# A third decision tree served by fetched rows, and a pipeline that carries the finish of each block into the next one

## The chip, the cores and the metric

One Trainium2 chip; the program runs on one of its NeuronCores. That core has TensorE (PE, 128x128 matmuls into PSUM), VectorE (DVE), ScalarE (ACT), GpSimd (POOL), and SyncE (SP), which here only issues DMAs. Each engine has its own instruction stream, in order, and the streams meet only at semaphores. The metric is the device time of one execution in microseconds (us): 1904.74 us for the kernel before, the median of 3 runs (1904.01 to 1905.8).

## The reference, cut to what matters

```
x = x + attn(layernorm(x))                  # x: 8192 tokens x 512
x = x + ffn(layernorm(x))

attn: q, k, v = x W^T + b, each turned into its unit spectrum f / (|f| + eps)
      out = ifft( cumsum_over_tokens(k_hat * v_hat) * conj(q_hat) )

ffn:  logits = x @ W_in.T + b_in            # 8 trees x 255 nodes
      decisions = logits > 0, acts = silu(logits)
      for d in range(7): follow the decision from the current node to a child
      dmap = one-hot of the 8 nodes visited in each tree (7 inner, 1 leaf)
      out = (acts * dmap) @ W_out.T
```

Only 8 of a tree's 255 nodes count for a token. The 127 inner logits are needed to find the path; of the 128 leaves only one is used.

## The kernel before

The 8192 tokens go through in 32 blocks of 256 (`T`), each as two halves `j` of 128. The first, the last two and the 29 in the middle (a hardware loop) run the same `step(i, attn, nxt)` on every engine; `first()` is the prologue (loading, folding a DFT into the projection weights, splitting all weights into an fp16 high and low part, block 0's attention up to its inverse transform). Each fp32 product is three fp16 matmuls (high*high, high*low, low*high).

In step `i`, with `n = i + 1`, PE does:

- `project(n, q)` for Q, K, V: 144 matmuls of 256 columns into `bank_p`, which yield the next block's spectra;
- `logits(i, t, c)`: for tree `t` 12 matmuls of 256 columns for the inner nodes (`c = 0`) and 12 for the leaves (`c = 1`), into `bank_l[t % 4]`, mixed with `counts(i, t)` (2 matmuls, which add a large negative number to every node off the path). Trees in `GATHERED` have no dense leaves: `counts` leaves in the free half of the bank a mark of the leaf reached, `leaf` and `leaf_rows_of` turn it into a row number, and POOL fetches that leaf's input row, bias and output row from HBM (`fetch`, 2 indirect DMAs a tree and block, one for each half). DVE then does `leaf_dots`, ACT `leaf_silu`, DVE `leaf_add`;
- `down(i, j)`: for each half and each of the `DENSE` column groups (14 here) 3 matmuls of 512 columns, into `bank_l[j]`;
- `transform_back(i)`: the inverse transform of block `n` into `bank_i`, 24 small matmuls.

Meanwhile the others do, for block `i`: `residual` (unfold the transform and add x: DVE), `stats`, `normalise`, `high`/`low` (layer norm and its split, ACT and DVE), two DMA transposes that give `x2t`, the input of `logits(i)`; then for each tree `decide` (DVE), `silu` and `act_high` (ACT), `act_low` (DVE). For block `n` they do `evac_*`, `square`, `root` (ACT), `sum_squares`, `add_eps` (POOL), `q_inverse`, `kv_inverse`, `k_scale` (DVE), `bind` (POOL), `running_sum` (DVE), `unbind`, `z_sums`, `z_low` (POOL); and for block `i + 2` the first layer norm. Nothing but the written order of each engine's list and the semaphores sets the order. `silu` writes to three SBUF buffers (`HELD = 3`), so a logit bank is free again once ACT has read it: `logits` of tree 4 and later wait for `act_ready`. `result` (the sum of `down`, the leaf rows and `x1`) ends DVE's step, and SP then stores it.

## Time and profile before

| | |
|---|---|
| median of the runs | 1904.74 us |
| profiled execution | 1902.03 us, of it 1899.9 us from the first to the last instruction |
| granted TensorE clock | 0.989 of full, on average |
| busy | PE 97%, DVE 82%, ACT 59%, POOL 50% |
| one step in the steady part | 56.3 us, 29 alike |
| the chain that ended last | 90% PE |

The profile comes from one execution. Busy time is given per engine; a group of instructions is named by its source line, engine, operation and tiles. "Idle before" says how long the engine stood just before such an instruction, and which instruction it had waited for. Start times count from the first instruction. Successive instructions overlap a little, so the pitch from start to start is shorter than the length given for one.

### The profile page before, as it was taken

What the parts mean: (1) busy time and instruction counts of PE and PEld (TensorE: products, weight loads), DVE (VectorE), ACT (ScalarE), POOL (GpSimd) and SP (SyncE); (2) the same over time, 40 slices, a digit from 0 to 9 for tenths busy, and PEclk for the clock granted to TensorE, in tenths of its full rate; (3) what the DMA queues carried; (4) which work ended last, traced back from release to release, by engine and by line L of the source; (5) the groups of instructions that cost most, each with busy time, mean ns of one, the idle gap of its engine ahead of it and who ended that gap; (6) DMA issues with size and microseconds to landing.
All of it is one profiled execution on the core that took longest, in us unless ns stands there. A gap on an engine that the chain in (4) does not pass through costs nothing.

```text
span 1899.9 us, 40007 instructions
## 1 busy us (share of the span) xinstructions
PE 1846.0 (97%) x14488; PEld 1389.5 (73%) x14488; DVE 1548.9 (82%) x2938; ACT 1117.4 (59%) x2151; POOL 943.0 (50%) x737
## 2 busy tenths in 40 slices
PE   8499999999999999999999999999999999999978
PEld 6478777778777778877777877777877777787755
DVE  4888888888888888888888888888888888888783
ACT  5666565566565556656556656556655555665643
POOL 1254445564445565444556445556544556545450
PEclk9799999999999999999999999999999999999999
DMA  8032232222133222223222213322223322222312
GB/s 288 12 87 79 68 100 92 74 88 88 55 100 100 70 85 88 73 82 100 79 87 87 85 59 100 98 68 88 88 59 96 100 77 77 88 69 86 89 56 67
DMA packets 181785, 163.18 MB, mean 86 GB/s; under 512 B 140161, under 2 KB 140801, under 8 KB 181761
## 3 DMA queue, kind: packets, MB, share of 16 engines
q1 hardware_dynamic: 163328, 95.48, 17.0%
q0 software_dynamic: 18432, 67.38, 10.7%
q8 instruction: 15, 0.25, 0.1%
q14 instruction: 10, 0.07, 0.0%
HBM read 95.72 MB, written 16.78 MB: 59 GB/s over the span
## 4 chain that ended last, share of the span: by engine, by line
PE 90%; DVE 2%; DMA 1%; ACT 1%; issue 0%; SPq 0%; DVEq 0%; ACTq 0%
PE bank_l L532 31%; PE bank_l L589 30%; PE bank_p L482 23%; PE bank_l L542 3%; PE bank_i L482 2%; DMA arena<-xn_pair 1%; PE bank_i L553 1%; PE bank_i L560 0%; SPq L341 0%; DVE xn_pair L1126 0%; DVE arena L1239 0%; ACT xn_pair L721 0%; ACT arena L794 0%; PE bank_i L559 0%; DVE arena L1249 0%
## 5 line engine op out<-in xcount | busy, mean ns | idle before, releaser
L532 PE MATMUL bank_l<-arena,win_mem 128*128 128x256 f16 x5376 | 625.1, 273 | 16.5 <-DMA arena<-xn_pair 16.5
L589 PE MATMUL bank_l<-wout_mem,arena 128*128 128x512 f16 x2688 | 593.4, 379 | 0.0
L532 PEld LDWEIGHTS bank_l<-arena,win_mem 128*128 128x128 f16 x5376 | 525.0, 98 | 80.5 <-DMA arena<-xn_pair 15.1
L482 PE MATMUL bank_p<-arena,wf_hi 128*128 128x256 f16 x3072 | 505.8, 273 | 2.7 <-ACT arena L740 2.7
L589 PEld LDWEIGHTS bank_l<-wout_mem,arena 128*128 128x128 f16 x2688 | 260.6, 98 | 308.8 <-DVE arena L1226 11.7
L482 PE MATMUL bank_p<-arena,wf_lo 128*128 128x256 f16 x1536 | 419.0, 273 | 0.0
L985 POOL TENSOR_TENSOR arena<-arena 128x512 f32<-128x512 f32 x96 | 121.8, 1269 | 553.1 <-ACT arena L749 553.1
L482 PEld LDWEIGHTS bank_p<-arena,wf_hi 128*128 128x128 f16 x3072 | 299.6, 98 | 37.6 <-ACT arena L740 3.0
L1226 DVE SCALAR_TENSOR_TENSOR arena<-arena,s_act 128x512 f16<-128x512 f32 (+1 forms) x256 | 238.7, 942 | 80.4 <-ACT arena L804 66.3
L794 ACT ACTIVATE arena<-bank_l,bias_in,s_logit 128x256 f32<-128x256 f32 x448 | 229.2, 554 | 121.4 <-PE bank_l L542 121.0
L1219 DVE TENSOR_SCALAR dec<-bank_l,thr,off 128x256 bf16<-128x256 f32 x256 | 136.0, 542 | 92.5 <-PE bank_l L532 91.0
L1066 POOL DMA_INDIRECT arena<-in_leaf_rows,leaf_row x128 | 140.3, 1096 | 109.4 <-issue 70.5
L804 ACT ACTIVATE arena<-arena,s_act 128x512 f16<-128x512 f32 (+1 forms) x256 | 166.6, 664 | 3.2
L482 PEld LDWEIGHTS bank_p<-arena,wf_lo 128*128 128x128 f16 x1536 | 150.5, 98 | 17.5
L1136 DVE RECIPROCAL arena<-arena 128x256 f32<-128x256 f32 x64 | 111.9, 1748 | 61.8 <-POOL arena L990 61.8
L1126 DVE TENSOR_TENSOR xn_pair<-arena,xn_pair 128x512 f16<-128x512 f32 x128 | 143.3, 1142 | 9.5 <-ACT xn_pair L721 9.5
L1239 DVE SCALAR_TENSOR_TENSOR arena<-arena 128x512 f32<-128x512 f32 x128 | 142.7, 1167 | 0.9 <-DMA arena<-in_leaf_rows,leaf_row 0.9
L990 POOL TENSOR_SCALAR arena<-arena,eps_s 128x512 f32<-128x512 f32 x64 | 45.4, 709 | 133.3 <-ACT arena L753 130.3
L1148 DVE RECIPROCAL arena<-arena 128x256 f32<-128x256 f32 x64 | 107.7, 1725 | 1.1
L714 ACT ACTIVATE arena<-arena 128x512 f16<-128x512 f32 x31 | 19.5, 630 | 149.1 <-POOL arena L1030 149.1
L726 ACT ACTIVATE arena<-bank_p,bias_f 128x256 f32<-128x256 f32 x192 | 80.5, 470 | 42.0 <-PE bank_p L482 42.0
L749 ACT ACTIVATE arena<-arena 128x1024 f32<-128x1024 f32 x96 | 101.5, 1057 | 5.3
(175 smaller groups left out, 2500.6 us busy)
## 6 DMA issues: line engine op xcount, KB each, us to landing
arena<-in_x SPq DMA_DIRECT2D x32, 512.0 KB, 3.5
arena<-arena SPq DMA_DIRECT2D x32, 512.0 KB, 2.9
out<-arena SPq DMA_DIRECT2D x64, 256.0 KB, 2.1
wout_mem<-in_w_in_t SPq DMA_DIRECT2D x1, 3584.0 KB, 16.1
arena<-in_w_out_t SPq DMA_DIRECT2D x1, 3584.0 KB, 13.8
arena<-xn_pair SPq DMA_TRANSPOSE x128, 2.8
arena<-in_leaf_rows,leaf_row POOLq DMA_INDIRECT x128, 5.7
win_mem<-in_wq SPq DMA_DIRECT2D x1, 1024.0 KB, 7.5
```

What stands on the lines that cost most here:

```text
L482: mm = pe.matmul(bank, a, b, start=(n == 0), stop=(n == len(pairs) - 1))
L532: mm = pe.matmul(bank_l[t % 4][:, c * T:(c + 1) * T], a[:, k, w:w + P], x2t[:, :, b, k, :], start=(c == 0 and k == 0 and m == 0), stop=((t ...
L589: mm = pe.matmul(bank_l[j][:, :], a[:, m, tok], w[:, m, :], start=(m == 0 and a is a_hi and w is wout_hi), stop=(m == DENSE - 1 and a is a ...
L794: ins = act.activation(acts[:, t % HELD, c * T:(c + 1) * T], bank_l[t % 4][:, c * T:(c + 1) * T], ACT.Silu, bias=bias_in[:, c, t:t + 1], s ...
L804: act.activation(a_hi[:, m:m + wide, :], acts[:, t % HELD, 0:wide * T].rearrange("p (c t) -> p c t", c=wide), ACT.Copy, scale=s_act[:, 0:1 ...
L985: pool.tensor_tensor(mag[:, q].rearrange("p c t -> p (c t)"), sq[:, 0:2].rearrange("p c t -> p (c t)"), sq[:, 2:4].rearrange("p c t -> p ( ...
L1066: pool.indirect_dma_start(fetched[:, g, j, :], None, leaf_rows, bass.IndirectOffsetOnAxis(leaf_row[:, g, j:j + 1], 0)).then_inc(leaf_fetch ...
L1126: dve.tensor_tensor(xn_pair[:, j, 1, :], xn[:, j, :], xn_pair[:, j, 0, :], ALU.subtract).then_inc(done, 1)
L1136: dve.reciprocal(mag[:, Q, h], mag[:, Q, h]).then_inc(rinv_ready, 1)
L1219: dve.tensor_scalar(dec[:, t % HELD, :], bank_l[t % 4][:, 0:T], thr[:, t:t + 1], off[:, 0:1], ALU.is_gt, ALU.mult).then_inc(dec_ready, 1)
L1226: dve.scalar_tensor_tensor(out=a_lo[:, m, :], in0=acts[:, t % HELD, 0:wide * T].rearrange("p (c t) -> p c t", c=wide), scalar=s_act[:, 0:1 ...
L1239: ins = dve.scalar_tensor_tensor(out=row, in0=row, scalar=1.0, in1=xn2[:, j, :], op0=ALU.mult, op1=ALU.mult, accum_out=leaf_dot[:, g, j:j ...
```

## The change: what it does

- `GATHERED` goes from two trees to three: tree 2 loses its dense leaf columns, `DENSE` goes from 14 to 13, and there are 6 indirect DMAs a step instead of 4, and three calls each of `leaf`, `leaf_dots`, `leaf_silu` and `leaf_add`.
- `acts` is gone: `silu` writes back into its PSUM bank, `act_high` and `act_low` read there, and a logit bank is free only when `a_lo_ready` comes.
- The normalised `xn2` lives in PSUM (`bank_i`) too; `keep_row` (ACT) copies it to `kept` for the dot products. The sum of x1 and leaf rows is begun by `begin_total` (ACT) in `bank_l[2]`, `bank_l[3]`.
- DVE's `leaf_add` (3) and `result` (2) of block `i` move from the end of step `i` into step `i + 1`, among `residual`, `stats`, `normalise` and `low`; a `last()` does them for block 31.
- The order of the projections is K, V, Q; SP transposes `x2t` ahead of the loads; `fetch` stands behind `z_sums` and ahead of `z_low` on POOL.
- `down(i, 1)` is called in two pieces, with `transform_back` behind both.
- The prologue does K and V before Q, and applies Q's inverse size to the products.

```diff
-GATHERED = (0, 1)
+GATHERED = (0, 1, 2)
-ROUNDS = ((0, 1),)
+ROUNDS = ((0, 1, 2),)
-Q, K, V, G_IN, G_OUT = range(5)
+K, V, Q, G_IN, G_OUT = range(5)
...
-        xn2 = take(J * D).rearrange("p (j d) -> p j d", j=J)
+        kept = take(J * D).rearrange("p (j d) -> p j d", j=J)
...
-        acts = take(HELD * 2 * T).rearrange("p (r t) -> p r t", r=HELD)
+        xn2 = [bank_i[j][:, :] for j in range(J)]
+        total = [bank_l[2 + j][:, :] for j in range(J)]
...
                 if c == 0 and t >= 4:
-                    pe.wait_ge(act_ready, TREES * i + t - 3)
+                    pe.wait_ge(a_lo_ready, TREES * i + t - 3)
                 elif c == 0 and (not isinstance(i, int) or i):
                     if t < J:
                         pe.wait_ge(y_ready, J * (i - 1) + t + 1)
                     else:
-                        pe.wait_ge(act_ready, TREES * (i - 1) + 5 + t)
+                        pe.wait_ge(leaf_added, LEAVES * i)
...
         def step(i, attn, nxt):                 # PE
                 if attn:
-                    project(n, Q)
                     project(n, K)
                     project(n, V)
+                if attn:
+                    project(n, Q)
                 logits(i, 0, 0)
                 logits(i, 1, 0)
                 counts(i, 0)
+                logits(i, 3, 0)
                 logits(i, 2, 0)
-                logits(i, 2, 1)
-                logits(i, 3, 0)
                 logits(i, 3, 1)
                 counts(i, 1)
+                counts(i, 2)
+                if attn:
+                    nyquist_rows(n)
                 logits(i, 4, 0)
...
-                down(i, 0)
-                down(i, 1)
+                down(i, 0, range(TREES))
+                if attn:
+                    nyquist_sums(n)
+                down(i, 1, range(0, 6))
+                down(i, 1, range(6, TREES))
                 if attn:
                     transform_back(i)
...
+            def keep_row(n, j):                  # ACT
+                act.activation(kept[:, j, :], xn2[j], ACT.Copy).then_inc(xn2_kept, 1)
+            def begin_total(i, j):
+                act.wait_ge(a_lo_ready, TREES * i + 7 + j)
+                act.activation(total[j], x1[:, j, :], ACT.Copy).then_inc(total_begun, 1)
...
-                    ins = act.activation(acts[:, t % HELD, c * T:(c + 1) * T], bank_l[t % 4][:, c * T:(c + 1) * T],
+                    ins = act.activation(bank_l[t % 4][:, c * T:(c + 1) * T], bank_l[t % 4][:, c * T:(c + 1) * T],
...
         def step(i, attn, nxt):                 # ACT, from tree 7 on
+                begin_total(i, 0)
                 if nxt:
+                    std(n + 1, mv1, rs1, ln1_mv, ln1_std)
+                if attn:
+                    z_high(n)
+                if nxt:
+                    shifted(n + 1)
                     high(n + 1, xn1, ln1_done, xn1_hi_ready)
-                act_high(i, 7)
-                if attn:
-                    z_high(n)
                 leaf_silu(i, 0)
                 leaf_silu(i, 1)
+                begin_total(i, 1)
+                leaf_silu(i, 2)
...
         def step(i, attn, nxt):                 # POOL
+                    bind(n)
                     q_unit(n)
-                    bind(n)
-                fetch(i, 1)
-                fetch(i, 0)
-                if attn:
                     unbind(n)
                     z_sums(n)
+                for g in range(LEAVES):
+                    fetch(i, g)
+                if attn:
                     z_low(n, 0)
                     z_low(n, 1)
...
         def step(i, attn, nxt):                 # DVE
+                if begun:
+                    leaf_add(i - 1, 0)
+                residual_of(i, 0)
+                residual_of(i, 1)
+                stats2(i)
+                if isinstance(i, int) and i == 0:
+                    win_low(3)
+                normalise2(i)
+                if begun:
+                    leaf_add(i - 1, 1)
+                low2(i)
+                if begun:
+                    leaf_add(i - 1, 2)
+                    result(i - 1, 0)
+                    result(i - 1, 1)
+                if attn:
+                    kv_denominator(n)
+                    kv_inverse(n, 0)
+                decide(i, 0)
+                if attn:
+                    kv_inverse(n, 1)
+                    k_scale(n)
+                decide(i, 1)
+                decide(i, 2)
+                act_low(i, 0)
+                if attn:
+                    q_inverse(n, 0)
+                    q_inverse(n, 1)
+                act_low(i, 1)
+                if attn:
+                    nyquist_den(n)
+                act_low(i, 2)
...
                 leaf_dots(i, 0)
                 leaf_dots(i, 1)
-                leaf_add(i, 0)
                 if attn:
                     carries(n)
-                leaf_add(i, 1)
-                result(i, 0)
-                result(i, 1)
+                leaf_dots(i, 2)
```

DVE, from the layer norm's statistics of block i to the first work for block n, before and after. L1107/L1192 is `normalise`, L1126/L1198 `low`, L1333 `leaf_add`, L1371 `result`, L1136 `q_inverse`, L1222 the K and V denominator.

```order
L1104 RECIPROCAL rs<-rs 128x2 [waits ln2_std]
L1107 TENSOR_SCALAR arena<-arena,mv,rs 128x512 [waits ln2_rstd]
L1107 TENSOR_SCALAR arena<-arena,mv,rs 128x512
L1126 TENSOR_TENSOR xn_pair<-arena,xn_pair 128x512 [waits xn2_hi_ready] x2
L1135 ISA
L1136 RECIPROCAL arena<-arena 128x256 [waits den_ready]
```

```order
L1189 RECIPROCAL rs<-rs 128x2 [waits ln2_std]
L1192 TENSOR_SCALAR bank_i<-arena,mv,rs 128x512 [waits ln2_rstd]
L1192 TENSOR_SCALAR bank_i<-arena,mv,rs 128x512
L1326 REGISTER_ALU
L1333 SCALAR_TENSOR_TENSOR bank_l<-arena,leaf_act,bank_l 128x512 [waits leaf_added,leaf_act_ready]
L1333 SCALAR_TENSOR_TENSOR bank_l<-arena,leaf_act,bank_l 128x512
L1198 TENSOR_TENSOR xn_pair<-bank_i,xn_pair 128x512 [waits xn2_hi_ready] x2
```

Two `leaf_add` instructions of the block before now stand between `normalise` and `low`.

PE, in the middle of the classification: the matmuls of trees 4 and 5 (L544 `logits`, L554 `counts`, L562 a small product) after the change, and then DVE from `decide` of tree 2 on (L1299 `decide`, L1306 `act_low` of trees 0, 1 and 2, L1216 `q_inverse`).

```order
L544 MATMUL bank_l<-arena,win_mem 128x256 [waits a_lo_ready]
L544 MATMUL bank_l<-arena,win_mem 128x256 x23
L544 MATMUL bank_l<-arena,win_mem 128x256 [waits a_lo_ready]
L544 MATMUL bank_l<-arena,win_mem 128x256 x11
L552 REGISTER_ALU
L554 MATMUL bank_l<-dec,path 128x256 [waits dec_ready]
```

```order
L1299 TENSOR_SCALAR dec<-bank_l,thr,off 128x256 [waits count_full,logit_full]
L1306 SCALAR_TENSOR_TENSOR arena<-bank_l,s_act,arena 128x256 [waits a_hi_ready]
L1216 RECIPROCAL arena<-arena 128x256 [waits den_ready] x2
L1306 SCALAR_TENSOR_TENSOR arena<-bank_l,s_act,arena 128x256 [waits a_hi_ready]
L1241 TENSOR_TENSOR sp_den<-bank_p,eps_sp 128x6 [waits sp_abs_ready]
L1306 SCALAR_TENSOR_TENSOR arena<-bank_l,s_act,arena 128x256 [waits a_hi_ready]
```

Before, tree 4's and 5's matmuls waited for `act_ready`; now tree 5's wait for the second of these `act_low`, which stands behind both reciprocals.

POOL, the end of a step, after the change. L1074 and L1075 are `z_sums`, L1120 `fetch`, L1082 `z_low`.

```order
L1074 TENSOR_TENSOR arena<-arena 128x512 [waits z_prod]
L1075 TENSOR_TENSOR arena<-arena 128x512
L1104 ISA
L1120 DMA arena<-in_leaf_rows,leaf_row 128x1028 [waits leaf_added,leaf_row_ready,consts_done]
L1120 DMA arena<-in_leaf_rows,leaf_row 128x1028
L1104 ISA
L1120 DMA arena<-in_leaf_rows,leaf_row 128x1028 [waits leaf_added,leaf_row_ready,consts_done]
L1120 DMA arena<-in_leaf_rows,leaf_row 128x1028
L1104 ISA
L1120 DMA arena<-in_leaf_rows,leaf_row 128x1028 [waits leaf_added,y_stored,leaf_row_ready,consts_done]
L1120 DMA arena<-in_leaf_rows,leaf_row 128x1028
L1080 REGISTER_ALU [waits z_sum]
```

Before, 4 fetches stood between `bind` and `unbind`; now 6 stand behind `z_sums`, and `z_low` behind them.

## Rows read from the trace of the kernel before

**Rows 1.** Head and first part of the profile's page: share of the span.
```profile
span 1899.9 us, 40007 instructions
PE 1846.0 (97%) x14488; PEld 1389.5 (73%) x14488; DVE 1548.9 (82%) x2938; ACT 1117.4 (59%) x2151; POOL 943.0 (50%) x737
```

**Rows 2.** Waits, whole run: who waited for whom, us, times, longest.
```profile
PE bank_l L532 <- DMA arena<-xn_pair: 16.5, 5, 14.1
PE bank_i L482 <- DVE arena L1399: 6.4, 1, 6.4
```

**Rows 3.** Timeline of PE: start, us, instruction (first, one step, last step).
```profile
109.41 2.78 PE L532 MATMUL bank_l<-arena,win_mem 128*128 128x256 f16 x24
...
938.71 0.38 PE L482 MATMUL bank_p<-arena,wf_hi 128*128 128x256 f16 x2
...
954.43 2.78 PE L532 MATMUL bank_l<-arena,win_mem 128*128 128x256 f16 x24
...
995.02 0.38 PE L482 MATMUL bank_p<-arena,wf_hi 128*128 128x256 f16 x2
...
1856.38 4.47 PE L532 MATMUL bank_l<-arena,win_mem 128*128 128x256 f16 x24 [14.11 <-DMA arena<-xn_pair]
```

**Rows 4.** The chain of waits in order of time: two of its pieces.
```profile
938.87 15.72 PE bank_p L482 x144
...
978.18 15.64 PE bank_l L589 x72
```

**Rows 5.** Timeline of DVE: the same step, and block 31.
```profile
946.42 0.25 DVE L1100 BATCH_NORM_AGGREGATE mv<-st 128x2 f32<-128x6 f32 x2
...
948.03 1.00 DVE L1107 TENSOR_SCALAR arena<-arena,mv,rs 128x512 f32<-128x512 f32 x2
949.33 1.29 DVE L1126 TENSOR_TENSOR xn_pair<-arena,xn_pair 128x512 f16<-128x512 f32 x2 [0.30 <-ACT xn_pair L721]
...
960.22 3.37 DVE L1148 RECIPROCAL arena<-arena 128x256 f32<-128x256 f32 x2
...
972.56 1.39 DVE L1199 TENSOR_TENSOR_SCAN arena<-arena,carry 128x256 f32<-128x256 f32 x2
...
995.61 0.28 DVE L1266 SCALAR_TENSOR_TENSOR arena<-bank_i,sp_z,odd 128x64 f32<-128x64 f32 x1 [0.32 <-ACT odd L906]
...
1851.42 1.29 DVE L1126 TENSOR_TENSOR xn_pair<-arena,xn_pair 128x512 f16<-128x512 f32 x2 [0.24 <-ACT xn_pair L721]
```

**Rows 6.** Timeline of ACT: the same step.
```profile
947.50 0.29 ACT L694 ACTIVATE rs<-mv,ln_eps 128x2 f32<-128x2 f32 x1
...
958.55 0.63 ACT L753 ACTIVATE arena<-arena 128x512 f32<-128x512 f32 x1 [0.22 <-POOL arena L985]
959.20 1.28 ACT L794 ACT_TABLE_LOAD   x1
960.50 0.56 ACT L794 ACTIVATE arena<-bank_l,bias_in,s_logit 128x256 f32<-128x256 f32 x1
```

**Rows 7.** Groups by shape: xcount | busy us, mean ns of one | idle before.
```profile
L1249 DVE SCALAR_TENSOR_TENSOR arena<-arena,leaf_act 128x512 f32<-128x512 f32 x128 | 92.4, 762 | 0.5 <-ACT leaf_act L782 0.4
L761 ACT ACTIVATE on_leaf<-bank_l,one,off_inv 128x256 f16<-128x256 f32 x64 | 35.6, 556 | 74.5 <-PE bank_l L542 74.5
L804 ACT ACTIVATE arena<-arena,s_act 128x256 f16<-128x256 f32 x64 | 31.9, 498 | 0.0
L1226 DVE SCALAR_TENSOR_TENSOR arena<-arena,s_act 128x256 f16<-128x256 f32 x64 | 30.8, 482 | 6.1 <-ACT arena L804 6.1
```

**Rows 8.** Timeline of POOL: unbind, second sum, low part of z; a fetch.
```profile
975.63 1.05 POOL L1066 DMA_INDIRECT arena<-in_leaf_rows,leaf_row  x1 [0.30 <-issue]
976.69 1.28 POOL L1018 TENSOR_TENSOR arena<-arena 128x512 f32<-128x512 f32 x1
...
986.77 2.99 POOL L1037 TENSOR_TENSOR arena<-arena 128x512 f16<-128x512 f32 x2 [0.74 <-ACT arena L714]
```

**Rows 9.** The page's DMA part: us from issue to landing.
```profile
arena<-in_leaf_rows,leaf_row POOLq DMA_INDIRECT x128, 5.7
```

More of the change, by code:

```diff
@@ L310, in build, with steps @@
         out_v = out.rearrange("(b j p) d -> b p j d", j=J, p=P)
-        def steps(eng, first, step):
+        def steps(eng, first, step, last=None):
             first()
@@ L323, in steps @@
             step(NB - 1, False, False)
+            if last is not None:
+                last()
         def chunks(flat):
@@ L376, in first @@
                     transpose(j, xt, xt_ready)
+                for j in range(J):
+                    sp.wait_ge(xn2_lo_ready, j + 1)
+                    transpose(j, x2t, x2t_ready)
             def held(value):
@@ L398, in step @@
                     sp.dma_start(xa, x_v[n + 1]).then_inc(x_loaded, 16)
-                for j, have in enumerate((first, second)):
-                    sp.wait_ge(consts_done, 1)
-                    if not isinstance(i, int) or i:
-                        sp.wait_ge(logit_full, classified)
-                    sp.wait_ge(xn2_lo_ready, have)
-                    if isinstance(i, int) and i == 0:
-                        sp.wait_ge(wout_hi_done, 1)
-                        sp.wait_ge(wout_lo_done, 1)
-                    transpose(j, x2t, x2t_ready)
-                if nxt:
                     for j in range(J):
@@ L416, in step @@
                         transpose(j, xt, xt_ready)
-                for j, have in enumerate((first, second)):
+                if attn:
+                    for j in range(J):
+                        sp.wait_ge(consts_done, 1)
+                        sp.wait_ge(logit_full, classified)
+                        sp.wait_ge(xn2_lo_ready, split2[j])
+                        transpose(j, x2t, x2t_ready)
+                for j in range(J):
                     sp.wait_ge(consts_done, 1)
-                    sp.wait_ge(y_ready, have)
+                    sp.wait_ge(y_ready, results[j])
                     sp.dma_start(out_v[i][:, j, :], y[:, j, :]).then_inc(y_stored, 16)
@@ L1544, in step, with last @@
                     carries(n)
-                leaf_add(i, 1)
-                result(i, 0)
-                result(i, 1)
-            steps(dve, first, step)
+                leaf_dots(i, 2)
+            def last():
+                for g in range(LEAVES):
+                    leaf_add(NB - 1, g)
+                result(NB - 1, 0)
+                result(NB - 1, 1)
+            steps(dve, first, step, last)
 def constants():
```

490 lines of the change are left out of this document (268 added, 222 removed).

## The prediction

> **What bounds the kernel now.** Start with the page's first lines [rows 1]: PE is busy 1846.0 of 1899.9 us, the next engine, DVE, 1548.9. Then ask for the waits [rows 2]: in the whole run PE waited 16.5 us for the transposed input of the classification (`x2t`), 14.1 of them in one place, block 31. So in the steady part PE is packed, and its own work is the bound. The timeline of PE gives the step: from 938.71 to 995.02, 56.31 us [rows 3]. The reader is to see there that no row of that step has an idle time in brackets.
>
> How near are the others? Let T0 be the start of the projections (938.71). `low` starts at 949.33 [rows 5], T0+10.62. Block 31 shows how long it takes from there to the first matmul that reads `x2t`, as nothing else held PE: 1851.42 [rows 5] to 1856.38 [rows 3], 4.96 us. So `x2t` was usable at T0+15.58, and PE came for it at 954.43 [rows 3], T0+15.72. This margin of 0.14 us is the most important number here: whatever is put in front of `low` becomes a wait of PE.
>
> **What the change takes off PE.** A matmul of 256 columns costs 15.72/144 = 0.109 us, one of 512 columns 15.64/72 = 0.217 us [rows 4]. The dense leaves of tree 2 were 12 of the first and 6 (two halves, three products) of the second: 1.31 + 1.30 = 2.61 us a step, 83.5 us over 32 steps. Two more tiny row-number matmuls are below 0.1 us. A packed PE would have a step of 53.7 us.
>
> **Wait one: x2t.** Up to the statistics nothing gets earlier: ACT takes the root for the layer norm only after the third evacuation, which PE paces (947.50 [rows 6], T0+8.8), though the statistics have been there since 946.67 [rows 5]. `normalise` then runs from T0+9.32 for 1.00 us. Now two `leaf_add` instructions follow, 92.4/128 = 0.7 us each [rows 7], 1.4 together, and then `low`. Of this 0.30 hides in DVE's former wait for `high` [rows 5]; so `low` begins 1.1 later, if `normalise` is as fast into PSUM as into SBUF. No row before shows a large DVE write into PSUM. Nearest below is its present half of 1.00 us; nearest above is `leaf_add`'s 0.7. I take 0.15 us a piece more, 0.3 for both, since `leaf_add` is what an instruction of this size costs at the ordinary rate. `x2t` comes at T0+15.58+1.4 = T0+17.0: PE waits 1.3 us, bounds 0.9 to 1.6.
> This agrees with a rule of the Trainium skill (VectorE: DVE Perf Modes, "Why PSUM operands drop a tier"), by which an fp32 instruction with a PSUM operand has no double rate. The trace's 1.00 us for two SBUF `normalise` is the fast side; the slow side has no row here. By the rule the wait is 1.3 us, without it 1.0.
>
> **Wait two: tree 5.** A logit bank is now given back only by `act_low`. The order on DVE is `act_low` 0, both `q_inverse`, `act_low` 1, and PE's first matmul of tree 5 waits for the last. Its time follows from rows, because Q now takes the last place that V had: ACT's last root starts at 958.55 (T0+19.84) [rows 6], held by PE's last projection, not by the logits. Then `leaf` for tree 0, which now stands behind it (pitch about 0.5, long 0.556), table load 1.28 with `silu` right behind (959.20, 960.50 [rows 6]), so `silu` starts at T0+22.25 and ends at T0+22.8; `act_high` 0.50 to T0+23.3; `act_low` pitch 0.40 to T0+23.75 [rows 7]; two reciprocals 3.37 [rows 5] to T0+27.1; `act_low` 0.48 to T0+27.55. When does PE come? Seven groups of 12 logit matmuls (84), 6 of `counts` and 4 small ones lie between `x2t` and tree 5: 94 at 0.109, 10.3 us, so T0+26.0 packed and T0+27.3 behind wait one. The gate at T0+27.55 counts from T0 and swallows the first wait: together they cost 27.55-26.0 = 1.55 us a step. Both ends: 1.0 (the gate vanishes, wait one stays) and 2.2 (`act_high` and the two `act_low` each 0.2 slower from PSUM than their rows from SBUF). I take the rows as they are, since `silu` and `decide` read PSUM already at like lengths.
>
> **Leaf rows and z, the long way round on POOL.** `running_sum` stands behind `act_low` 1 and 2 and `decide` 3 and 4 (0.4 to 0.5 each), so it starts at about T0+29.0 and, at twice 1.39 less their overlap [rows 5], ends at T0+31.65. Then unbind and both sums, 976.69 to 986.03 (986.77 less the 0.74 idle): 9.34 us [rows 8], to T0+41.0. The 6 fetches at 1.05+0.30 us [rows 8] end at about T0+49.2; `z_low`, 2.99, at T0+52.3. PE wants z at the new T0' minus 1.35, about T0+53.9: hidden by 1.6 us. The last fetch is issued at T0+48.1 and lands 5.7 later [rows 9], T0+53.8; its two dot products and then `leaf_add` 0, four instructions at 0.65 to 0.7 [rows 7], end at T0+56.5. With T0' = T0+55.25 the residual starts at T0'+1.25, where it was T0+0.6 (995.61 against 995.02 [rows 5]); the statistics end at T0'+8.6, just ahead of ACT's root at T0'+8.8. So this chain costs nothing, with 0.2 us to spare; each us beyond that reaches `x2t` in full, and PE once it exceeds the 0.25 by which the gate lies behind PE.
>
> **Others.** DVE: two more dot products and two more adds at 0.7 [rows 7], 2.8 us a step, less 0.4 for the narrower `act_low`; its 82% becomes about 88%. It fits, and `result` (now at T0+14.6 to 15.9) frees banks 0 and 1 before PE is there. ACT gains a leaf mask, two `keep_row`, two `begin_total` and, because the first layer norm's root now stands behind the `silu`s, two more table loads: 2.6 us at 1.28 [rows 6]; it falls in the long `down`, where I count ACT ready for the leaf dots at T0+47.2. The Trainium skill (ScalarE: Activation LUTs, "What ACT_TABLE_LOAD costs") adds a drain of 1.38 us to each load. The trace disagrees: after 959.20 the next instruction starts 1.30 later [rows 6], so the load alone counts. The `x2t` transposes leave SP ahead of the loads: no change. `down` in two calls with the transform behind both issues the same list as one; nothing.
>
> **Prologue and ends.** PE started the next block's classification at 109.41 [rows 3], after 6.4 us of waiting for the low part of z [rows 2]. With K and V first, the binding overlaps Q's folding and projection; adding up the list (8 tiles, K, a tile, V, 3 tiles, Q, then running sum, products, reciprocals, z) I estimate the first transform about 9 us earlier. But the output weights' split, which was done before and beside it, now stands inside block 0's classification: ACT's and DVE's eight pieces of about 2 us put some 4.7, 3.3 and 2 us of waits into PE. Net of both about +2 us; bounds -5 and +8. In block 31 no projection covers the chain to `x2t`: 14.1 us [rows 2] becomes about 16, +2.
>
> **Sum**, against the profiled execution (1899.9 span, 1902.03 with what lies around it): -83.5 + 30 x 1.55 (46.5) + 2 + 2 = -33, 1869. The median of the runs was 2.7 above that execution; I forecast 1904.7 - 33 = 1871.7, say 1871.
>
> **Rivals.**
> 1. *The waits vanish, PE stays packed.* The two gates are sums of a dozen pitches; 1.5 us off on both, or a DVE that gets through `q_inverse` sooner, frees PE. For: DVE had no wait in PE's way before. Against: the margin of 0.14 us is measured, and two `leaf_add`s are longer. Time: 1904.7 - 83.5 + 4 = 1825; with half the waits 1848. Chance 0.25 for below 1850.
> 2. *Slower: the row fetches come too late.* Place: POOL between `z_sums` and `z_low`, DVE's dots, and `leaf_add` 0 in front of the residual. The margin is 0.2 us. If the fetches take 1.6 instead of 1.35 us each, or POOL's sums are slowed by DVE's new work, the chain is 1.5 to 3 us late; PE then waits 1.0 to 2.6 us more a step. It decides from 1.1 us a step on: there 53.7+1.55+1.1 reaches 56.3. At 3 us late the time is 1871 + 30 x 2.6 = 1949; at 1.5 late 1900. For: the margin is thin, and six fetches stand in a row. Against: the POOL rows repeat from step to step, and DVE reads more from PSUM than before, so it shares less with POOL. Chance 0.12 for slower.
> 3. *The change does not do what it says*: the transform is not inside the `down` products in PE's list. It costs nothing, since z was to be hidden anyway; no chance of its own.
>
> **Chances.** Forecast (1850 to 1893) 0.60; packed or nearly 0.25; same 0.03; slower 0.12. No change would be within 0.2%, 1901 to 1908.5. Faster 0.85, same 0.03, slower 0.12. The range for 8 in 10: 1826 to 1895; the forecast's own is 1850 to 1893.
>
> **What would show it.** In a steady step of the new profile: 54.5 to 56 us from T0 to T0'; PE waits of about 1.3 us at the first `logits` (released by the DMA transposes) and 0.3 us at tree 5 (released by `act_low`); four table loads a step on ACT; `z_low` ending more than 1 us before the transform; `leaf_add` 0 ending about 1 us after T0'. Wrong is it if PE has no waits there (rival 1), or if the residual starts over 2 us after T0' or PE waits at the transform (rival 2).

## The result: slower, and the profile after

The changed kernel takes 2066.07 us (median of 4 runs, 2062.06 to 2072.64); the kernel before took 1904.38 on the same chip. The ratio is 1.0852, with a 95% interval of 1.0834 to 1.0871. The forecast was 1871 us in a range of 1826 to 1895: the kernel became slower where it was to become faster, and the time is 195 us off.

The page of the changed kernel, its head, its queues and its landings (they answer to [rows 1] and [rows 9]):

```profile
span 2060.4 us, 39784 instructions
PE 1822.3 (88%) x13976; PEld 1359.5 (66%) x13976; DVE 1564.6 (76%) x3130; ACT 1250.3 (61%) x2403; POOL 924.4 (45%) x801
...
q1 hardware_dynamic: 163200, 94.96, 22.1%
q0 software_dynamic: 27648, 101.07, 17.4%
...
arena<-in_leaf_rows,leaf_row POOLq DMA_INDIRECT x192, 8.3
arena<-xn_pair SPq DMA_TRANSPOSE x128, 3.3
```

No engine is busier than before in share; even PE fell from 97% to 88%. So the time is in waits. Note the last two lines: a row fetch now lands after 8.3 us where it took 5.7 [rows 9]. The transposes' median of 3.3 hides the point, since it is taken over all 128. Half of them are for the classification (`x2t`), half for the next block's projection (`xt`), and the stretch below shows that the latter are slow.

The waits of the whole run (who waited for whom: us, times, longest), where [rows 2] had 16.5 and 6.4 us in all for PE:

```profile
DVE arena L1320 <- DMA arena<-in_leaf_rows,leaf_row: 200.2, 35, 8.4
PE bank_p L491 <- DMA arena<-xn_pair: 132.3, 29, 6.4
PE bank_l L544 <- DMA arena<-xn_pair: 64.6, 31, 16.0
```

The third row is the forecast wait for `x2t`. The second is new and was in no part of the forecast: in 29 steps PE waits 4.6 us (132.3/29) for the transposed input of the *projection*, `xt`. The first shows the rows late as well. One step in the timeline, engine by engine (it answers to [rows 3], [rows 5] and [rows 8]). T0, the start of its projections, is 1015.66:

```profile
1015.66 0.39 PE L491 MATMUL bank_p<-arena,wf_hi 128*128 128x256 f16 x2 [1.72 <-DMA arena<-xn_pair]
1033.44 2.79 PE L544 MATMUL bank_l<-arena,win_mem 128*128 128x256 f16 x24 [1.72 <-DMA arena<-xn_pair]
1077.42 0.61 PE L491 MATMUL bank_p<-arena,wf_hi 128*128 128x256 f16 x2 [5.93 <-DMA arena<-xn_pair]
...
1025.28 1.53 DVE L1192 TENSOR_SCALAR bank_i<-arena,mv,rs 128x512 f32<-128x512 f32 x2
1043.23 0.38 DVE L1306 SCALAR_TENSOR_TENSOR arena<-bank_l,s_act,arena 128x256 f16<-128x256 f32 x1
1076.64 0.69 DVE L1320 SCALAR_TENSOR_TENSOR arena<-arena 128x512 f32<-128x512 f32 x1 [8.06 <-DMA arena<-in_leaf_rows,leaf_row]
...
1056.63 1.01 POOL L1120 DMA_INDIRECT arena<-in_leaf_rows,leaf_row  x1
1062.91 1.44 POOL L1120 DMA_INDIRECT arena<-in_leaf_rows,leaf_row  x1 [0.30 <-issue]
...
1062.89 5.37 SPq L348 DMA_TRANSPOSE arena<-xn_pair  x2
```

See how the last three rows lie. POOL issues its six fetches from 1056.63 to 1064.35; SP issues the two transposes at 1062.89, in the midst of them. PE can start with `xt` at 1077.42, 14.5 us after that issue. (Its wait of 5.93 is one of the longer ones; they go from 1.4 to 6.4 us.) The step is 61.76 us long here, and over the 28 steps from 210.96 to 1939.82 it is 61.75 on average (56.31 before). What the DMA engines did in that stretch (1056 to 1078), packets, bytes and landings:

```profile
DMA packets 2976, 3.68 MB, mean 167 GB/s; under 512 B 2208, under 2 KB 2208, under 8 KB 2976
q0 software_dynamic: 864, 3.16, 51.5%
q1 hardware_dynamic: 2112, 0.52, 38.0%
arena<-in_leaf_rows,leaf_row POOLq DMA_INDIRECT x6, 10.7
arena<-xn_pair SPq DMA_TRANSPOSE x2, 13.3
```

And the same view of the kernel before, in the like stretch of its step (970 to 992):

```profile
q0 software_dynamic: 576, 2.11, 28.2%
q1 hardware_dynamic: 2112, 0.52, 10.6%
arena<-in_leaf_rows,leaf_row POOLq DMA_INDIRECT x4, 5.8
arena<-xn_pair SPq DMA_TRANSPOSE x2, 2.7
```

The same two transposes, 2112 packets and 0.52 MB both times, took 10.6% of a 22 us stretch and now take 38.0%. Worked out from these shares of 16 engines, one of their packets took 18 ns before and takes 63 now, while one of the row fetches' went only from 172 to 210. Before, the last fetch was issued at 975.63 [rows 8] and landed 5.7 us later, 3.7 us before SP issued the transposes (984.99).

The waits also cost clock. Three projections (144 matmuls each) that began after waits of 1.72, 5.93 and 5.86 us, in stretches (start and end, length, busy time of each engine, then granted clock, DMA share, GB/s):

```profile
1015.60:1033.40 17.80, 16.06 (x144) 13.92 (x144) 16.91 (x43) 13.57 (x28) 3.24 (x3) 1.00 0.20 47
1077.40:1096.50 19.10, 17.54 (x144) 14.87 (x145) 16.92 (x43) 13.53 (x28) 3.25 (x3) 0.91 0.19 43
1140.40:1160.40 20.00, 18.45 (x144) 15.30 (x144) 16.73 (x43) 13.55 (x28) 3.25 (x3) 0.87 0.18 41
```

After the long wait the first matmuls take 0.61 us a pair where they take 0.39 at the full clock of 2.4 GHz: the granted clock is 0.50 of full in the microsecond from 1077.42, its lower level of 1.2 GHz, and comes back within the projection. In such a step that is 1.5 to 2.4 us (17.54 and 18.45 against 16.06 busy) beside the wait itself. Of the 29 waits at this place, 17 were followed by a first pair at the lower clock: 15 of the 16 from 5.0 us up, 2 of the 13 below.

### The profile page after: what moved, and what is told of

Its sections match the earlier page's. It is cut to its first block and busy times, and to the rows that moved or that the text cites. A ratio compares the mean times of both kernels' runs of the same rounds, so it can differ in the third digit from the quotient of the medians.

```text
span 2060.4 us, 39784 instructions
## 1 busy us (share of the span) xinstructions
PE 1822.3 (88%) x13976; PEld 1359.5 (66%) x13976; DVE 1564.6 (76%) x3130; ACT 1250.3 (61%) x2403; POOL 924.4 (45%) x801
## 5 line engine op out<-in xcount | busy, mean ns | idle before, releaser
L491 PE MATMUL bank_p<-arena,wf_hi 128*128 128x256 f16 x3072 | 553.6, 288 | 134.3 <-DMA arena<-xn_pair 132.3
L544 PE MATMUL bank_l<-arena,win_mem 128*128 128x256 f16 x4992 | 583.7, 274 | 68.3 <-DMA arena<-xn_pair 64.6
L544 PEld LDWEIGHTS bank_l<-arena,win_mem 128*128 128x128 f16 x4992 | 483.7, 99 | 138.2 <-issue 54.3
L1320 DVE SCALAR_TENSOR_TENSOR arena<-arena 128x512 f32<-128x512 f32 x192 | 190.8, 1040 | 200.2 <-DMA arena<-in_leaf_rows,leaf_row 200.2
L834 ACT ACTIVATE bank_l<-bank_l,bias_in,s_logit 128x256 f32<-128x256 f32 x416 | 210.8, 537 | 148.9 <-PE bank_l L554 148.5
L1120 POOL DMA_INDIRECT arena<-in_leaf_rows,leaf_row x192 | 196.1, 1022 | 101.1 <-issue 46.3
L1306 DVE SCALAR_TENSOR_TENSOR arena<-bank_l,s_act,arena 128x512 f16<-128x512 f32 (+1 forms) x256 | 161.2, 631 | 39.5 <-ACT arena L844 39.4
L826 ACT ACTIVATE leaf_act<-leaf_dot,arena 128x1 f32<-128x1 f32 x192 | 43.0, 284 | 219.5 <-DVE arena L1320 214.0
L844 ACT ACTIVATE arena<-bank_l,s_act 128x512 f16<-128x512 f32 (+1 forms) x256 | 156.6, 612 | 5.3
L1299 DVE TENSOR_SCALAR dec<-bank_l,thr,off 128x256 bf16<-128x256 f32 x256 | 134.5, 536 | 20.0 <-PE bank_l L544 14.6
L1216 DVE RECIPROCAL arena<-arena 128x256 f32<-128x256 f32 x64 | 107.3, 1718 | 0.0
L1180 DVE TENSOR_TENSOR xn_pair<-arena,xn_pair 128x512 f16<-128x512 f32 x64 | 46.0, 721 | 78.2 <-issue 73.0
## 6 DMA issues: line engine op xcount, KB each, us to landing
arena<-in_w_out_t SPq DMA_DIRECT2D x1, 3328.0 KB, 13.7
```

The costliest lines, as they stand in the source:

```text
L491: mm = pe.matmul(bank, a, b, start=(n == 0), stop=(n == len(pairs) - 1))
L544: mm = pe.matmul(bank_l[t % 4][:, c * T:(c + 1) * T], a[:, k, w:w + P], x2t[:, :, b, k, :], start=(c == 0 and k == 0 and m == 0), stop=((t ...
L834: ins = act.activation(bank_l[t % 4][:, c * T:(c + 1) * T], bank_l[t % 4][:, c * T:(c + 1) * T], ACT.Silu, bias=bias_in[:, c, t:t + 1], sc ...
L844: act.activation(a_hi[:, m:m + wide, :], bank_l[t % 4][:, 0:wide * T].rearrange("p (c t) -> p c t", c=wide), ACT.Copy, scale=s_act[:, 0:1] ...
L1120: pool.indirect_dma_start(fetched[:, g, j, :], None, leaf_rows, bass.IndirectOffsetOnAxis(leaf_row[:, g, j:j + 1], 0)).then_inc(leaf_fetch ...
L1216: dve.reciprocal(mag[:, Q, h], mag[:, Q, h]).then_inc(rinv_ready, 1)
```

## The experiments

All are edits of the changed kernel. Theory T: the six fetches' bytes and the two `xt` transposes are in the 16 DMA engines at once, and both are late. The rivals are named in each expectation. The kernels of experiments 1 and 5 leave half of each row unfetched and serve only to read the time.

**1. Half rows.**

```
-  indirect_dma_start(fetched[:, g, j, :], None, leaf_rows, ...)
+  # from block 1 on: 514 of a row's 1028 words
+  indirect_dma_start(fetched[:, g, j, 0:ROW // 2], None, leaf_rows.rearrange("r (a w) -> (r a) w", a=2), ...)
```

> The changed kernel, but from block 1 on each of the six row fetches of a step brings 514 of a row's 1028 words (so the leaves' dots and sums are taken over rows that are partly old: the output is not the reference's). The number of fetches, their place on POOL and every instruction elsewhere stay; the bytes fall from 3.16 to 1.58 MB a step. Theory T (the six fetches' bytes share the 16 DMA engines with the two transposes of the next block's rows, which then land after 9 to 14 us, and the projection waits for them 4.6 us a step, with a slower TensorE clock behind it): the projection's wait falls under 1 us a step, the period from 61.8 to 56 to 57.5 us, the whole to about 1900 us (1880 to 1940). Rival A (the new order of the next layer norm's high and low halves and of x2t's transposes makes the transposes late, whatever the traffic): no change, within 10 us of 2066. Rival B (the number of gather instructions on the software queue, not their bytes): no change either, 2040 to 2070.

Measured: 1879.65 us (1872.57 to 1881.12), 0.9869 of before (0.9848 to 0.9891). The larger group of the projection (count, busy us, mean ns, idle before) and the wait at `x2t`:

```profile
L491 PE MATMUL bank_p<-arena,wf_hi 128*128 128x256 f16 x3072 | 509.2, 274 | 5.9 <-DMA arena<-xn_pair 3.9 <-issue 1.9
```

```profile
PE bank_l L544 <- DMA arena<-xn_pair: 63.5, 31, 16.0
```

In the changed kernel this group read 553.6, 288 and 134.3 idle. With six fetches in the same place and every instruction elsewhere kept, only the bytes halved: the projection's wait went from 132.3 to 3.9 us, and its matmuls went back from 288 to 274 ns. In the stretch from 1028 to 1050 the two transposes landed after 4.2 us (median), where they took 13.3. The period is 55.4 us (from `x2t` to `x2t`, 1005.15 to 1060.51). Between the two profiled spans lie 181.5 us: 128.4 less idle time before the projection, and 48.0 less busy time of PE (1822.3 to 1774.3), the clock's part. T holds; rivals A and B would have left the time alone. Time and period came out just below T's ranges (1880 to 1940, and 56 to 57.5).

**2. Fetches ahead of z's products again,** with the next layer norm's high halves ahead of `z_high`:

```
 POOL:  bind; q_unit
+       fetch x6
        unbind; z_sums
-       fetch x6
        z_low
 ACT:   leaf_row_copy behind act_high(3), was behind silu(6); high(n + 1) before z_high(n), was after
```

> The changed kernel with the fetches of the leaf rows back where the kernel before had them, ahead of z's products on POOL (the copy of the row numbers behind the fourth act_high, about T0+30), and the next layer norm's high halves ahead of z_high on ACT. Still three trees by row, six fetches, 3.16 MB. Theory T: fetches are over before the two transposes are issued, which land in about 3 us; the projection does not wait, TensorE's clock stays at 1.00, the period is 55 to 56.5 us, the whole 1860 to 1900 us. Rival A': three trees by row are too many bytes wherever they stand: the transposes still wait, or the rows, and the whole stays over 1950. Rival C: z is late instead, because eight microseconds of POOL stand ahead of its products, and the transform waits: 1920 to 2000.

Measured: 1965.25 us (1953.48 to 1970.65), 1.0340 (1.0323 to 1.0358). The projection's wait is gone and its clock back at 1.00, as T says, but the time lies 65 us above T's range, for another wait. The number falls into the ranges of rivals A' and C, but neither mechanism is there: PE waits for no transpose at the projection and not at all at the transform. What it does wait for:

```profile
DVE dec L1299 <- remote: 80.9, 31, 3.1
PE bank_l L554 <- DVE dec L1299: 64.7, 26, 2.7
```

```profile
1060.49 0.75 DVE L1306 SCALAR_TENSOR_TENSOR arena<-bank_l,s_act,arena 128x512 f16<-128x512 f32 x1 [0.25 <-issue]
1064.23 0.54 DVE L1299 TENSOR_SCALAR dec<-bank_l,thr,off 128x256 bf16<-128x256 f32 x1 [2.99 <-remote]
```

DVE stands still for 3 us (1.6 to 3.1 in other steps) ahead of the eighth tree's comparison, though that tree's last logit matmuls ended at 1060.23, as the row of PE says:

```profile
1058.76 1.47 PE L544 MATMUL bank_l<-arena,win_mem 128*128 128x256 f16 x12
```

The profile can name no releaser ("remote" stands for one that it does not know). The semaphore updates in the trace say more: the comparison waits for a count (a semaphore) that PE's last logit matmul raises, and this count rose only at 1064.21, 3.98 us after the matmul's end (which the profile models) and 0.02 before the comparison. In the 31 steps with this stall the count came 2.3 to 4.0 us late. So VectorE waits for a late count of PE. Experiments 5, 6, 7 and 11 go after it.

**3. The transposes held back until the rows have landed.**

```
 SP, before the xt transposes:
+  sp.wait_ge(leaf_fetched[0..2], 16 * J * (i + 1))
```

> The changed kernel with SP holding the two transposes of the next block's rows back until the step's six row fetches have landed. Theory T (they share the engines, nothing else): the rows land earlier than 10 us after their issue (6 to 8), the transposes 3 to 4 us after theirs, and the projection starts at about the time at which it starts now or up to 3 us earlier: 1980 to 2080 us. Rival A (transposes are issued too late, they are slow for a reason of their own): every transpose still takes 9 us or more from its issue, and the whole rises by 29 times 6 to 8 us, to over 2220.

Measured: 1977.41 us, 1.0395 (1.0374 to 1.0416): 89 us *faster* than the changed kernel, by making the transposes wait, and 3 us below T's range. The rows' landing, and one step (fetches from 1075.28):

```profile
arena<-in_leaf_rows,leaf_row POOLq DMA_INDIRECT x192, 6.3
```

```profile
1075.28 1.01 POOL L1125 DMA_INDIRECT arena<-in_leaf_rows,leaf_row  x1 [0.16 <-issue]
...
1087.92 2.62 SPq L348 DMA_TRANSPOSE arena<-xn_pair  x2
...
1092.50 0.39 PE L496 MATMUL bank_p<-arena,wf_hi 128*128 128x256 f16 x2 [2.36 <-DMA arena<-xn_pair]
```

One after the other, the rows need 12.6 us from the first fetch's issue (1087.92 less 1075.28) and the transposes 4.6 more, 17.2 in all. Side by side they needed 20.8 in the step shown above (1056.63 to 1077.42). Over all steps the same stretch, from the first fetch to the projection, is 17.5 us long here and 19.4 in the changed kernel, where it varies from 16.2 to 21.2. So mixed, they lose 1.9 us on average, though not in every step: "they share the engines, nothing else" is not the whole of it. Rival A falls: a transpose has no slowness of its own.

**4. High halves first, fetches left late.** The ACT edit of experiment 2 alone (`high(n + 1)` ahead of `z_high(n)`).

> The changed kernel with the next layer norm's high halves ahead of z_high on ACT, as in the kernel before; the fetches stay between z's sums and z's low part. Rival A (the transposes are issued too late): they are issued 2 to 3 us earlier, the projection's wait falls from 4.6 to about 2 us and the whole to 1990 to 2010. Theory T: the transposes are issued earlier and fall into the middle of the fetches, and land hardly earlier; the wait stays over 3.5 us and the whole is 2030 to 2070.

Measured: 2067.85 us, 1.0870 (1.0835 to 1.0905), within its spread the changed kernel's time; the projection's wait was 128.6 us. It is what T expected, but a weak test: one step shows the transposes issued 5.85 us after the first fetch (1059.26 less 1053.41) instead of 6.26 (1062.89 less 1056.63), so the edit moved them by 0.4 us and not by the 2 to 3 that I had assumed. They were read 14.7 us after their issue (1073.98), as late as before. So this run does not test rival A; experiment 3 does.

**5. Experiment 2 with half rows.**

> The kernel of the second experiment (row fetches ahead of z's products) with half rows from block 1 on (514 of 1028 words; the output is not the reference's). There the eighth tree's comparison on VectorE started 3 us late in every step (2.99 us idle, released by an unknown queue) and PE waited 2.7 us for it. Theory D (the stall comes of the 3.16 MB on the DMA engines): it is gone or under 0.5 us, the period 55.4 us, the whole 1870 to 1885. Theory G (it comes of GpSimd's issuing six fetches, whose number and time stay): it stays at 2 to 3 us, the period 58, the whole 1950 to 1970.

Measured: 1871.14 us, 0.9834 (0.9814 to 0.9853). No stall at the comparison; PE's waits there are the 6.0 us of the first steps. Theory D holds: the stall of experiment 2 comes with the bytes, not with issuing fetches. PE's count for the eighth comparison rises 0.01 us after its matmul here in every step.

**6. The second sum over leaf rows behind the low halves** (experiment 2's kernel, full rows):

```
 DVE:   normalise2(i)
-       leaf_add(i - 1, 1)
        low2(i)
+       leaf_add(i - 1, 1)
```

> The kernel of the second experiment with the second sum over leaf rows moved behind both low halves of xn2 on VectorE, so that x2t's transposes can be issued some 1.5 us earlier. If the wait of 1.5 us at x2t is made of what stands ahead of these halves, it falls to 0.2 us or less and the period by 1.3 to 1.5: 1915 to 1930 us with the stall at the eighth comparison, 1830 to 1850 if that goes too. If instead something else ends last there (the normalisation into PSUM, the transposes themselves), it stays above 1 us and the time within 10 us of 1965.

Measured: **1864.68 us** (1864.11 to 1866.22), 0.9799 of before (0.9782 to 0.9815). This is the best kernel of the study, 1.9 to 2.2% faster than the kernel before. The stall is gone, with all bytes fetched. PE's waits and, for the step, its rows:

```profile
PE bank_l L544 <- DMA arena<-xn_pair: 25.0, 31, 14.7
PE bank_l L544 <- DVE arena L1306: 18.2, 32, 2.2
PE bank_l L554 <- DVE dec L1299: 15.9, 33, 2.2
```

```profile
995.89 2.79 PE L544 MATMUL bank_l<-arena,win_mem 128*128 128x256 f16 x24 [0.35 <-DMA arena<-xn_pair]
999.00 0.39 PE L554 MATMUL bank_l<-dec,path 128*128 128x256 bf16 x2 [0.32 <-DVE dec L1299]
...
1007.26 1.48 PE L544 MATMUL bank_l<-arena,win_mem 128*128 128x256 f16 x12 [0.52 <-DVE arena L1306]
```

The wait for `x2t` shrank from 1.5 to 0.35 us, as meant; but 0.32 and 0.52 us took its place (the comparison of tree 0, now behind more of DVE's work, and `act_low` 1 at tree 5's gate). The period is 55.27 us (median) where experiment 5, with the `x2t` wait whole, had 55.36. My range for "stall gone" (1830 to 1850) had counted the freed 1.3 us without asking what is late next.

**7. The row numbers' copy one `act_high` later,** in experiment 6's kernel.

> The kernel of the experiment before it with the copy of the row numbers behind the fifth act_high instead of the fourth, so that the six fetches start about 1.8 us later, still ahead of z's products. If the stall of the eighth comparison depends on how much of the traffic has been issued when it comes up, it shrinks to under 1.5 us and the whole falls by 40 us or more against that experiment; if it goes with the end of the fetches' issue, it grows by about 1.8 us and the whole rises by about 50 us. The transposes stay clear of the fetches in both cases (they were landed 4 us before PE came to them): no wait at the projection.

Measured: 1867.92 us, 0.9815 (0.9799 to 0.9831). Neither branch: there was no stall left to shrink or to grow. The fetches started only 1.4 us later (33.5 against 32.1 us behind T0, medians), and the 3 us in all lie within the overlap of the two intervals.

**8. The rows held back until the transposes have landed,** `z_low` ahead of them on POOL.

```
 POOL:  unbind; z_sums; z_low
+       wait_ge(xt_ready, 16 * J * (n + 2))
        fetch x6
```

> The changed kernel with z's low part ahead of the fetches on POOL, and the fetches held back until the two transposes of the next block's rows have landed. Theory T (they slow each other on the shared DMA engines): the transposes land in 3 to 4 us and the projection does not wait (under 0.5 us a step), TensorE starts it at the full clock. The rows land 6 to 8 us after their issue, 10 us or so after the transform's start, the dots, the residual and x2t's transposes behind them on VectorE come 7 to 10 us late, and the wait moves to x2t: 6 to 10 us a step there, the whole 2030 to 2180 us. If the transposes still took 9 us or more with nothing beside them, theory T would be wrong.

Measured: 2228.97 us, 1.1714 (1.1691 to 1.1738), clock 0.92. The transposes took 3.2 us and PE no longer waits for them, as T says. The price of late rows is 49 us above the expected range, and it is paid in another place:

```profile
PE bank_p L491 <- ACT arena L770: 280.9, 30, 10.4
PE bank_l L544 <- DMA arena<-xn_pair: 66.6, 31, 21.2
```

```profile
1025.10 1.28 ACT L826 ACT_TABLE_LOAD   x1 [13.97 <-DVE arena L1322]
...
1033.68 0.82 ACT L770 ACTIVATE arena<-bank_p,bias_f 128x256 f32<-128x256 f32 x2
```

Late rows make late dots, `leaf_silu` stands on ACT ahead of everything of the next step, and ACT waits 13.97 us for them; its first evacuation of the projection's banks starts at 1033.68, and PE, out of banks, waits 9 us. It is not `x2t` that pays, but the projection.

**9. Two trees by row** in the changed kernel's order (four fetches, in the late place; tree 2 dense again).

```
-GATHERED = (0, 1, 2)        -ROUNDS = ((0, 1, 2),)
+GATHERED = (0, 1)           +ROUNDS = ((0, 1),)
```

> The changed kernel with two trees by row instead of three, as the kernel before had, and four fetches (2.11 MB) a step; they stay between z's sums and z's low part. Its x2t transposes of block 0 wait for one more scale, and the third tree's second half of logits is back on TensorE (2.6 us a step). If four fetches also collide with the transposes of the next block's rows, the projection waits 3 us or more and the whole is over 2040 us. If four are over in time (they start 6 us before the transposes and need 6 to 8 us of all engines), the wait is under 1 us and the period 55.4 and 2.6 us, 58: 1935 to 1965 us. That would say that neither the third tree nor the new place costs the 4.6 us alone, only both together.

Measured: 1956.93 us, 1.0283 (1.0263 to 1.0304). Two neighbouring steps:

```profile
926.73 2.79 PE L545 MATMUL bank_l<-arena,win_mem 128*128 128x256 f16 x24 [1.58 <-DMA arena<-xn_pair]
984.71 2.79 PE L545 MATMUL bank_l<-arena,win_mem 128*128 128x256 f16 x24 [1.59 <-DMA arena<-xn_pair]
```

The period is 58.0 us; PE waits 1.6 us a step at `x2t` and not at all at the projection. As expected, four fetches in the late place do no harm: the transposes are issued 7.7 us behind the first fetch, when the last has some 2 us to go, and both have landed 4.7 us later (4.5 in experiment 3). So neither the third tree nor the new place makes the 4.6 us alone. The third tree's dense leaves are 2.6 us of this period; without them it would be 55.4.

**10. Experiment 6's DVE edit alone,** fetches left late.

> The changed kernel with only the second sum over leaf rows behind the low halves of xn2. The wait at x2t goes from 1.5 to about 0.3 us a step. If the projection's start is set by the transposes (which follow the block's own logits on ACT and DVE, all of them shifted with PE), the whole falls by about 30 times 1.2 us less the waits of 0.8 us that took its place in the sixth experiment: 2040 to 2066 us, with the projection's wait still 4 us or more.

Measured: 2072.24 us, 1.0889 (1.0858 to 1.0921), where 2040 to 2066 was expected; it can't be told from the changed kernel's time. The wait for `x2t` fell to 25.3 us in the run and the projection's wait rose to 145.4: as long as the transposes set the step, nothing gained elsewhere counts.

**11. Experiment 2 with the copy one `act_high` later.**

> The kernel of the second experiment, where the eighth comparison on VectorE stalls 3 us in every step, with the row numbers' copy one act_high later (fetches start about 1.8 us later), and the sum over leaf rows not moved. If the stall comes of the full traffic at that instruction whatever its moment, it is there again and the whole is about 1965 us; if it needs a certain moment of the fetches against the comparison, it goes and the whole is 1870 to 1885 us (as with half rows).

Measured: 1915.43 us, 1.0067 (1.0051 to 1.0084): between the two numbers. The stall left DVE and appeared on ACT, ahead of the eighth tree's `silu`:

```profile
ACT bank_l L834 <- remote: 88.6, 29, 3.2
PE bank_l L599 <- DVE arena L1306: 28.0, 28, 1.1
```

3.1 us a step again (88.6/29), but ACT has room there, and PE pays 1.0 us of it. Again it is a count of PE that rises late, this time that of a `counts` matmul: 3.2 us late at 1044.08, for one that ended at 1040.87. In this step the count rose 8.5 us after the first fetch was issued, as in experiment 2 (8.5 there too), though the matmul ended 5.3 us after it and not 4.5.

**12. `act_low` 1 between the two reciprocals of q,** in experiment 6's kernel; `decide` 3 moves ahead of `act_low` 2 with it.

> The kernel of the sixth experiment (1864.7 us) with act_low of the second tree between the two reciprocals of q instead of behind both, and the fourth tree's comparison ahead of the third act_low. There PE waited 0.52 us a step for that act_low. If nothing is late in its place, the period falls by 0.3 to 0.5 us and the whole by 9 to 16 us, to 1849 to 1856; if the comparison behind the longer chain is late instead, it stays within 3 us of 1865.

Measured: 1869.57 us, 0.9828 (0.9812 to 0.9845): 5 us slower than experiment 6. The gate fell only from 0.52 to 0.42 us, and PE waited 18.2 us for comparisons in the run where experiment 6 had 15.9. So the gain of the first branch is not there, and the time is 2 us above what the second allowed. A count of PE is late here too, by 1.4 us in most steps, where experiment 6 has none; which of the two costs the 5 us is not shown.

## Why the prediction was wrong

- **The term that failed** is in "Leaf rows and z": "So this chain costs nothing, with 0.2 us to spare", with its landing of 5.7 us. The last rows were to land at T0+53.8, and the dot products that need them started at 1076.64, T0+60.98. The issue was not late: fetches were to start at T0+41.0 and started at 1056.63, T0+40.97, and the last was issued at T0+47.25 where T0+48.1 was forecast. (The first agreement is luck. `unbind` began at 1048.61, T0+32.95, 1.3 us later than forecast, and with the sums took 7.9 us and not 9.34.) But 5.7 us was the landing of four fetches with the DMA engines to themselves; six beside two transposes landed after 10.7 (median), the last one after some 13.7. Experiments 1 and 3 show the cause both ways: PE's wait at the projection goes with half the bytes, and with the transposes out of the way the rows land after 6.3 us.
- **The term that was missing.** Under "Others" I asked only about the `x2t` transposes ("leave SP ahead of the loads: no change"). The `xt` transposes for the next block's projection, on which the start of every step hangs, were in no sum; in the prediction's terms, their landing was put at nothing. The trace of before had their time: SP issued them at 984.99, T0+46.3, and I had just put the fetches at T0+41 to T0+48 with the last landing at T0+53.8. So the overlap could be read before any run. It costs 4.6 us of wait a step, and PE's busy time is 48 us longer than in experiment 1, most of it slower clock behind the longer waits, which I had not counted either.
- **Rival 2 came nearest** (row fetches too late, by POOL's order; 0.12), and its number, up to 1949, was far too low, since it priced slow issuing and not slow landing. The rows were late (200.2 us of DVE's waits), but PE stood still for the transposes. Experiment 8 prices late rows by themselves, with the wait at the projection's evacuation and not, as the rival had it, at `x2t`.
- **PE's work removed, 2.61 us a step**: right. Experiment 9, which puts it back, has a period of 58.0 against experiment 1's 55.4.
- **Waits one and two, together 1.55 us**: the sum is right, its split is not, and that is in part luck. Experiment 1, where nothing else is late, has 1.5 to 1.6 us at `x2t` and nothing at tree 5 (1.3 and 0.25 were forecast), and a period of 55.4 where 53.7+1.55 = 55.25 was forecast. In the changed kernel wait one is 1.5 to 1.7 us. Its cause is right, but the term for `normalise` was too small: into PSUM it takes 1.53 us for two against 1.00 from SBUF to SBUF [rows 5], 0.53 more where 0.3 was put. The Trainium skill (VectorE: DVE Perf Modes, "Why PSUM operands drop a tier") says that an fp32 instruction with a PSUM operand gets no double rate; the trace agrees with the direction of that. Wait two's gate is there as well: `act_low` 1 ended at 1043.61, T0+27.95, where T0+27.55 was forecast, just as PE came to it behind the longer wait one. Once wait one is shortened (experiment 6) PE waits 0.52 us for the gate.
- **Block 31**, 14.1 to "about 16": 16.0. **Table loads**, two more on ACT at 1.28: right, and hidden. **Prologue**: the transform started at 77.79 instead of 87.41, 9.6 us earlier ("about 9"), and PE waited 9.6 us in block 0's classification for the weights' split (10.0 forecast).
- **`down` in two calls with the transform behind both** costs nothing: right; nothing waits there.
- **The sum** without the collision is near what experiments 1 and 5 measured, with half the rows' bytes: 1879.65 and 1871.14 against the 1871 forecast. The arithmetic of the engines held; the one shared resource that was never put in the sum turned the -1.8% of the forecast into +8.5%.

What stays open is the 3 us stall of experiments 2 and 11. Shown is that it is a count of PE that rises 2 to 4 us after its matmul, that it needs the full bytes (experiment 5), and that it holds up DVE or ACT depending on a shift of 1.8 us in the fetches (experiments 2 and 11). It does not arise with the same bytes at the same offset when the sum over leaf rows stands two instructions later. In experiment 6 the first fetch was issued at 1011.77 and the comparison ran at once, at 1017.24, 5.5 us behind it; in experiment 2 the first fetch was at 1055.68 and DVE was free for the comparison at 1061.24, 5.6 us behind. PE's count rose 0.01 us after the matmul in the first and 3.98 in the second, for matmuls that ended 4.5 us behind the first fetch in both. The kernel before has it in small, beside four fetches: in 29 of its steps one count of PE is 1.1 us late, and PE never waits there. Why the count is late is not shown.

## What to carry to other kernels

When transfers are moved or added, lay *every* transfer of the step out on one time line, those of other queues too, and ask which one an engine waits for: a landing time from the profile holds only beside the traffic it was measured in. A pair of small transposes on the critical path (0.52 MB here) matters more than the 3.16 MB beside it; keep the bulk transfers clear of it, if need be by holding one of the two back. And a short wait of PE costs more than its length once it lets the clock fall.

## What was not expected of the hardware

- The two DMA transposes (128x1024 fp16 each, 2112 packets and 0.52 MB together) land in 2.7 us alone and in 13.3 us beside six row fetches of 3.16 MB (4112 bytes a row). The fetches take 5.8 us (four, alone), 6.3 (six, alone, experiment 3) and 10.7 (six, beside the transposes). In turns both took 17.5 us on average, mixed 19.4. The Trainium skill (DMA: Bandwidth & Descriptors, "Queues, rings and completion order") says that each DMA engine takes turns between the queues it has work for, packet by packet. The trace fits that, as it is the small packets that suffer (18 to 63 ns each, the rows' 172 to 210), and with half rows the transposes take 4.2 us. No run here separates it from another way of sharing.
- A DVE leaf dot, with two operands in SBUF, takes longer beside a POOL `tensor_tensor`, but not beside the issue of a fetch. In the changed kernel it takes 0.68 us alone (135 of them), 0.68 beside nothing but an indirect DMA on POOL (26), and 2.9 on average where the low part of z runs beside it (29), as here:

```profile
1064.26 2.94 DVE L1320 SCALAR_TENSOR_TENSOR arena<-arena 128x512 f32<-128x512 f32 x1
...
1064.37 2.27 POOL L1082 TENSOR_TENSOR arena<-arena 128x512 f16<-128x512 f32 x2
```

- How often a wait of PE was followed by the lower clock (0.61 us for the first pair against 0.39): in 30 of 30 waits of 8.9 to 10.4 us (experiment 8), in 15 of 16 of 5.0 to 6.4 us (changed kernel), and in 5 of 30 of 2.2 to 3.4 us (experiment 3).
- A count that PE raises for another engine can arrive microseconds late while indirect fetches are in flight: 2.3 to 4.0 us in 31 steps of experiment 2, 1.1 us in 29 steps of the kernel before, and at most 0.01 us at the same matmul in experiments 5 and 6.
